# Attention with a position bias on one core: where the next batch's first stack stands in the DMA queue, and the softmax inversion one slot ahead

## The chip, the core and the metric

The kernel runs on one core of one Trainium2 chip. The metric is the device time of one launch in microseconds. The core has TensorE (PE), VectorE (DVE), ScalarE (ACT), GpSimd (POOL) and SyncE (SP), which issues nearly all transfers here, and 16 DMA engines that carry them.

## The reference

Sixteen batches of 512 tokens with 256 features go through a layer norm and then two branches, whose sum is added to x.

```python
xn = layernorm(x)                                   # (16, 512, 256)
q, k, v = split(xn @ w_qkv.T + b_qkv)               # 16 heads of 16
att = q @ k.T / 4 + hope_bias(pos_independent)      # per head, 512 x 512
att = softmax(where(causal, att, -inf))
attn = (att @ v) @ w_proj.T + b_proj
ffn = fp8_gemm(xn.astype(bf16), ffn_kernel)         # values rounded to float8_e4m3
out = x + attn + ffn
```

The bias of a head is a sum of cosines and sines of the distance i - j and a constant. It can therefore be written as a product of features of i and features of j, which the kernel stacks under q and k.

## The kernel before

**Stacks.** Each head has 64 rows in `STK`: high and low parts of q and k and the position features that belong to them. A *pair* of heads fills the 128 partitions of `STK[:, u]`, and a *stack* is the four heads (two pairs) of one group g of four. One transfer of 512 KB per pair copies it from 32 partitions of `QKP`, where the projections are written (line 365, `load_stack`, called once per batch and group; it signals `stack_loaded[g]` for both pairs).

**Units and slots.** A batch b has 4 units, one per group g, and a unit has 12 slots. In a slot PE does a tile of transposed scores of (b, g) (`scores_T`, line 629, and 632 for the position features of groups 0 and 1, kept in `EXT`) and, in turn with it, a tile of scores of the group two units further on (`scores`, line 606). The latter serve only to find the row maxima: DVE adds the causal mask and takes maxima (`chunk_max`, line 989). Twelve tiles later ACT rounds the maxima, PE turns them (line 590), ACT writes them as `neg_max_T` (line 830), and SP sends them, in four transfers of 4 KB, into two rows of each head's stack (line 328, `send_max`, `load_max`). So the transposed scores of (b, g) come out with the maximum already taken off, and ACT's exponential (line 911) writes the probabilities straight. POOL masks them (line 1187), PE multiplies them by V beside ones (line 655), so that the sums of the rows come along.

In unit 2 of batch b the scores ahead are those of (b+1, group 0). They need the next batch's first stack.

**Inversion.** The sums of all 16 heads are gathered in `DEN`. DVE inverts them in one instruction (line 996, `invert`) in unit 0 of the next batch, at the slot `INVERT_AT`, behind that slot's maxima. SP stores them to DRAM (`store_recips`, line 384), and reads them back spread over partitions (`spread_recips`, line 396, two transfers of 256 KB). POOL divides in unit 1.

**What sets the order.** Each engine's order is written out by hand: tables of (unit, slot) at the top of the file, and for SP the sequence in `body`. A queue is in order: SP waits for one condition, issues, and goes on. Within a batch SP does: the last stack of this batch, the maxima of group 1, `store_recips`, x for b+2, `spread_recips`, **the next batch's first stack, the maxima of group 2, the regrouping of `out_T` of group 0** (lines 341 and 342), the next batch's second stack, the maxima of group 3, and so on. The places where PE waits for it:

```python
# scores, at tile 0 of a unit
pe.wait_ge(stack_loaded[g], 32 * (b + 1))
# scores_T, at slot 0 of a unit
pe.wait_ge(max_loaded[g], 64 * (b + 1))
```

The first wait asks for both pairs of the stack (16 from each). In a slot the first transposed tile comes ahead of the tile of scores. At unit 2's slot 0 PE then does the quantised product (line 582).

Of the kernel before, what the change touches and what calls it, by code (L numbers as in the profile page):

```python
# [72 lines left out]
XH_AT, FIRST_XH_AT = [(3, 9), (3, 10)], [(0, 2), (0, 2)]  # L73
XL_AT, FIRST_XL_AT = [(3, 10), (0, 0)], [(0, 3), (0, 3)]

INVERT_AT, LAST_INVERT_AT = (0, 8), (3, 8)
STATS_AT, AGGR_AT = [(1, 2), (1, 3), (1, 5), (1, 8)], (1, 9)
MAGIC_AT = [(2, 0), (2, 1), (2, 2)]

# [48 lines left out]
def build(nc, x, w_qkv, b_qkv, w_proj, b_proj, pos, ffn_w, s_in, s_k, ffn_b, feat_q, feat_k, out):  # L128
    with ExitStack() as ctx:
# [196 lines left out]
        def send_max(eng, g):  # L326
            for h in range(HU):
                eng.dma_start(max_rows(g, h), MTS[2 * TT * h:2 * TT * h + 2 * TT, g % 2, :].bitcast(F32)) \  # L328
                    .then_inc(max_loaded[g], 16)

        def wait_alone(eng, always, *pairs):


            held = [(s, v if isinstance(v, int) else eng.compute_val(v)) for s, v in pairs]
            eng.wait_ge(*always)
            for s, v in held:
                eng.wait_ge(s, v)

        def send_attn(eng, b, g):
            r = 64 * (g % 2)  # L340
            eng.dma_start(attn_row(b)[r:r + HU * HD, g // 2, :], OT[0:P:2, :]).then_inc(ot_stored[g % 2], 16)
            eng.dma_start(DEN[32 * g:32 * g + 32, :], OT[1:P:2 * HD, :]).then_inc(den_loaded[g % 2], 16)
# [13 lines left out]
        def _(sp):  # L356
            def load_x(b):
                sp.dma_start(x_slot(b), x[bass.ds(b, 1), :, :].rearrange("o (t p) c -> p (o t) c", p=P)) \
                    .then_inc(x_loaded, 16)

            def load_stack(b, g):

                for u in (2 * g, 2 * g + 1):
                    r = 32 * (u % 4)
                    sp.dma_start(STK[:, u, :, :].bitcast(F32), QKP[r:r + 32, u // 4, :, :, :].bitcast(F32)) \
                        .then_inc(stack_loaded[g], 16)

            def load_max(b, g):
                sp.wait_ge(mts_ready, 4 * b + g + 1)
                send_max(sp, g)  # L370

            def regroup(b, g, early):

                if g == 0 and not early:

                    wait_alone(sp, (w_loaded, 16), (al_ready, b), (rc_ready, b), (ot_ready, 4 * b + g + 1))
                else:
                    sp.wait_ge(ot_ready, 4 * b + g + 1)
                send_attn(sp, b, g)

            def store_recips(b):

                wait_alone(sp, (w_loaded, 16), (rc_ready, b + 1), (rb_loaded, 32 * (b + 1)))
                sp.dma_start(recips.rearrange("h (e j) -> (h e) j", e=8), RDEN[:, :]).then_inc(rc_stored, 16)

            def spread_recips(b, last):

                if not last:

                    wait_alone(sp, (w_loaded, 16), (rc_stored, 16 * (b + 1)), (t_ready, 2 * (b + 3)))  # L390
                else:
                    sp.wait_ge(rc_stored, 16 * (b + 1))
                    sp.wait_ge(qm_done, 2 * B)
                for ct in range(CT):
                    src = recips[8 * ct:8 * ct + 8, :].unsqueeze(1).broadcast_to([8, HD, T])
                    sp.dma_start(RB[:, ct, :], src).then_inc(rb_loaded, 16)
# [50 lines left out]
            for u, loaded in enumerate((first_pair, stack_loaded[0])):  # L447
                sp.dma_start(STK[:, u, :, :].bitcast(F32), QKP[32 * u:32 * u + 32, 0, :, :, :].bitcast(F32)).then_inc(loaded, 16)
            load_stack(0, 1)
            sp.wait_ge(ql_ready, 4)  # L450
            sp.wait_ge(const_made, 2)
            load_stack(0, 2)
            load_low_features(1)

            def store_out(b):
                sp.wait_ge(out_ready, 2 * (b + 1))
                sp.dma_start(out[bass.ds(b - 1, 1), :, :].rearrange("o (t p) c -> p (o t) c", p=P),
                             x_slot(b + 3)).then_inc(out_stored, 16)

            def body(b, first, last, load):  # L460
                if not first:
                    sp.wait_ge(st_ready, ROW * b)
                load_stack(b, 3)
                load_max(b, 1)
                if not first:
                    store_recips(b - 1)
                if load:
                    if not first:
                        sp.wait_ge(out_stored, 16 * b)
                    sp.wait_ge(x_loaded, 16 * (b + 2))  # L470
                    load_x(b + 2)
                if not first:
                    spread_recips(b - 1, last)

                if not last:
                    wait_alone(sp, (w_loaded, 16), (st_ready, ROW * b + SLOTS),
                               (ql_ready, 4 * (b + 1) + 2))
                    load_stack(b + 1, 0)
                load_max(b, 2)
                regroup(b, 0, first)  # L480

                if not last:
                    wait_alone(sp, (w_loaded, 16), (st_ready, ROW * b + 2 * SLOTS))
                    load_stack(b + 1, 1)
                load_max(b, 3)
                regroup(b, 1, first)

                if not last:
                    wait_alone(sp, (w_loaded, 16), (st_ready, ROW * b + 3 * SLOTS),
                               (ql_ready, 4 * (b + 1) + 4))  # L490
                    load_stack(b + 1, 2)
                if not last:
                    load_max(b + 1, 0)
                regroup(b, 2, first)
                if not first and not last:
                    store_out(b)

            body(0, True, False, True)
            with sp.Fori(1, B - 2) as b:
                body(b, False, False, True)  # L500
            body(B - 2, False, False, False)
            body(B - 1, False, True, False)
            store_recips_of(0, 12, B)
# [846 lines left out]
```

## Time and profile before

| what | value |
|---|---|
| median of 3 runs | 822.24 us (822.04 to 825.26) |
| the profiled execution's own time | 820.26 us |
| its span, first to last instruction | 818.5 us |
| mean granted TensorE clock | 0.973 of full speed |
| PE busy | 747.2 us, 91% |
| DVE, ACT, POOL busy | 628.9, 581.0, 528.2 us |
| DMA, mean over the span | 130 GB/s |
| one batch, inversion to inversion | 46.4 to 47.6 us |

Busy time says how long an engine worked, not whether the work was on the path that sets the end. For that the profile has a chain of waits, followed back from the last instruction, and a list of who waited for whom. SP counts as a queue: the length of a DMA instruction on it is the time until the issue was accepted, and the time to landing is told apart.

### The profile page before, as it was taken

What the parts mean: (1) busy time and instruction counts of PE and PEld (TensorE: products, weight loads), DVE (VectorE), ACT (ScalarE), POOL (GpSimd) and SP (SyncE); (2) the same over time, 40 slices, a digit from 0 to 9 for tenths busy, and PEclk for the clock granted to TensorE, in tenths of its full rate; (3) what the DMA queues carried; (4) which work ended last, traced back from release to release, by engine and by line L of the source; (5) the groups of instructions that cost most, each with busy time, mean ns of one, the idle gap of its engine ahead of it and who ended that gap; (6) DMA issues with size and microseconds to landing.
All of it is one profiled execution on the core that took longest, in us unless ns stands there. A gap on an engine that the chain in (4) does not pass through costs nothing.

```text
span 818.5 us, 23154 instructions
## 1 busy us (share of the span) xinstructions
PE 747.2 (91%) x6313; PEld 510.0 (62%) x6313; DVE 628.9 (77%) x2395; ACT 581.0 (71%) x1258; POOL 528.2 (65%) x525
## 2 busy tenths in 40 slices
PE   6869999999999999999999999999999999999883
PEld 3546666666676667657676666657666666767552
DVE  3767878887977878788788878787787879778722
ACT  4236767777786877778687777778677777867671
POOL 6433568567666867667676757766685776667580
PEclk8859999999999999999999999999999999999998
DMA  6834666567566656666566657756665775666502
GB/s 170 165 68 95 114 145 123 129 148 144 127 138 153 118 130 138 138 145 137 141 121 151 123 127 162 142 126 137 148 117 123 155 143 124 139 130 121 120 24 86
DMA packets 55548, 106.07 MB, mean 130 GB/s; under 512 B 10464, under 2 KB 30432, under 8 KB 55520
## 3 DMA queue, kind: packets, MB, share of 16 engines
q1 hardware_dynamic: 53192, 102.96, 60.4%
q10 hardware_dynamic: 2328, 2.77, 1.0%
q8 instruction: 13, 0.21, 0.1%
q14 instruction: 15, 0.12, 0.0%
HBM read 18.68 MB, written 8.91 MB: 34 GB/s over the span
## 4 chain that ended last, share of the span: by engine, by line
PE 49%; ACT 15%; SPq 11%; issue 9%; DMA 7%; DVE 5%; ACTq 3%; DVEq 1%; POOL 0%; POOLq 0%
SPq L328 11%; PE misc_a L539 8%; PE misc_a L655 8%; PE scoreT_b L629 6%; PE misc_b L539 6%; ACT probs L911 6%; PE scoreT_a L629 3%; DMA stacks<-neg_max_T 3%; PE misc_b L655 3%; PE score_a L606 3%; PE score_c L606 2%; ACT qk_parts L818 2%; ACT out_T L884 2%; ACT attn_hi L893 2%; ACT xnT_hi L807 1%
## 5 line engine op out<-in xcount | busy, mean ns | idle before, releaser
L1187 POOL TENSOR_SCALAR_AFFINE_SELECT probs<-probs 128x512 f32<-128x512 f32 x256 | 159.5, 635 | 244.7 <-ACT probs L911 242.8
L989 DVE CUSTOM_DVE_ANT_0 score_b<-score_b,causal_mask_q 128x384 f32<-128x384 f32 (+3 forms) x321 | 161.9, 521 | 119.6 <-PE score_b L606 118.4
L989 DVE CUSTOM_DVE_ANT_0 score_a<-score_a,causal_mask_q 128x512 f32<-128x512 f32 x319 | 173.1, 559 | 8.1 <-PE score_a L606 4.1
L911 ACT ACTIVATE probs<-scoreT_b 128x384 f32<-128x384 f32 (+1 forms) x256 | 134.5, 525 | 60.7 <-issue 23.7
L989 DVE CUSTOM_DVE_ANT_0 score_c<-score_c,causal_mask_q 128x256 f32<-128x256 f32 (+3 forms) x384 | 171.4, 474 | 2.3 <-PE score_c L606 2.2
L911 ACT ACTIVATE probs<-scoreT_a 128x512 f32<-128x512 f32 (+1 forms) x256 | 145.6, 569 | 14.0 <-PE scoreT_a L632 7.4
L989 DVE DVE_READ_ACCUMULATOR2_ANT row_max<- 128x1 f32 x1024 | 142.9, 140 | 0.0
L911 ACT ACTIVATE probs<-scoreT_c 128x384 f32<-128x384 f32 (+1 forms) x256 | 136.2, 532 | 3.7 <-PE scoreT_c L632 3.3
L655 PE MATMUL misc_a<-probs,v_ones 128*32 128x128 f32 (+3 forms) x1536 | 131.2, 438 | 0.4 <-POOL probs L1187 0.4
L629 PE MATMUL scoreT_a<-stacks 64*128 64x512 f32 (+3 forms) x320 | 108.3, 358 | 21.8 <-DMA stacks<-neg_max_T 13.8
L629 PE MATMUL scoreT_b<-stacks 64*128 64x384 f32 (+3 forms) x320 | 119.5, 393 | 7.6 <-ACT probs L911 7.1
L606 PE MATMUL score_b<-stacks 64*128 64x384 f32 (+3 forms) x321 | 118.3, 401 | 0.3 <-DVE row_max L989 0.2
L629 PE MATMUL scoreT_c<-stacks 64*128 64x256 f32 (+3 forms) x384 | 105.7, 308 | 8.7 <-ACT probs L911 8.7
L606 PE MATMUL score_a<-stacks 64*128 64x512 f32 x319 | 108.5, 372 | 5.5 <-DVE row_max L989 4.0
L629 PEld LDWEIGHTS scoreT_b<-stacks 64*128 64x128 f32 x320 | 56.8, 185 | 73.5 <-ACT probs L911 42.5
L606 PE MATMUL score_c<-stacks 64*128 64x256 f32 (+3 forms) x384 | 99.2, 312 | 0.5 <-DVE row_max L989 0.2
L629 PEld LDWEIGHTS scoreT_c<-stacks 64*128 64x128 f32 x384 | 68.7, 186 | 16.0 <-ACT probs L911 14.1
L655 PEld LDWEIGHTS misc_a<-probs,v_ones 128*32 128x32 f32 x1536 | 59.7, 109 | 29.5 <-issue 13.3
L629 PEld LDWEIGHTS scoreT_a<-stacks 64*128 64x128 f32 x320 | 57.1, 186 | 30.8 <-DMA stacks<-neg_max_T 15.9
L606 PEld LDWEIGHTS score_a<-stacks 64*128 64x128 f32 x319 | 55.3, 188 | 22.1 <-DVE row_max L989 16.4
L606 PEld LDWEIGHTS score_c<-stacks 64*128 64x128 f32 x384 | 65.7, 189 | 5.1 <-DVE row_max L989 4.8
L884 ACT ACTIVATE out_T<-misc_a 128x512 f32<-128x512 f32 x48 | 28.7, 598 | 41.4 <-PE misc_a L655 39.8
(241 smaller groups left out, 1948.9 us busy)
## 6 DMA issues: line engine op xcount, KB each, us to landing
stacks<-qk_parts SPq DMA_DIRECT2D x128, 512.0 KB, 8.1
x_ring<-in_L_attn_x SPq DMA_DIRECT2D x16, 512.0 KB, 3.6
xn<-recips SPq DMA_DIRECT2D x31, 256.0 KB
out<-x_ring SPq DMA_DIRECT2D x15, 512.0 KB, 3.0
attn<-out_T SPq DMA_DIRECT2D x48, 128.0 KB, 2.6
stacks<-neg_max_T SPq DMA_DIRECT2D x128, 4.0 KB
attn<-out_T ACTq DMA_DIRECT2D x16, 128.0 KB, 2.9
low_features<-neg_max_T SPq DMA_DIRECT2D x124, 4.0 KB
```

Source lines behind the costliest of these rows:

```text
L328: eng.dma_start(max_rows(g, h), MTS[2 * TT * h:2 * TT * h + 2 * TT, g % 2, :].bitcast(F32)) \
L539: last = mm(o, l(ct), r(ct), start=(ct == 0 and i == 0), stop=(ct == CT - 1 and i == 2))
L606: last = mm(SB_[n % 3][:, o:o + w], STK[rows, u, 0, P * qt:P * qt + P], STK[rows, u, 1, 0:w], start=True, stop=True)
L629: last = mm(bank, STK[rows, u, 1, P * j:P * j + P], STK[rows, u, 0, P * j:T], start=True, stop=(g >= 2))
L655: last = mm(bank[32 * i:32 * i + 32, P * j:T], VA[:, j, HU * g + i, :, :].rearrange("p d a -> p (d a)"), probs(g, j)[:, i, :], start=(j == ...
L807: A(XH[:, ct, :], misc_of("T", ct)[:, :], ACT.Copy).then_inc(xh_ready, 1)
L818: A(qk_part(m, 0), misc_of("QK", m)[:, :].unsqueeze(1).broadcast_to([P, 2, T]), ACT.Identity, bias=BQ[:, bias:bias + 1]).then_inc(qh_ready, 1)
L884: A(OT[:, :], misc_of("PV", g)[:, :], ACT.Copy).then_inc(ot_ready, 1)
L893: A(AH[:, ct, :], attn_row(b)[:, ct, :], ACT.Copy).then_inc(ah_ready, 1)
L911: A(probs_slot(g, k), STB[(SLOTS * g + k) % 3][:, 0:w], ACT.Exp).then_inc(exp_done, 1)
L989: last = V.tensor_tensor_reduce(bank, bank, CMQ[:, T - w:T], 1.0, LEAST, ALU.add, ALU.max, MX[:, g % 2, 8 * h + 4 + qt:8 * h + 5 + qt])
L1187: last = GP.affine_select(out=d, in_=d, compare_op=ALU.is_ge, fill=0.0, base=0, pattern=[[0, HU], [1, P]], channel_multiplier=-1)
```

## The change

The next batch's first stack is sent in two steps. Its first pair (heads 0 and 1) goes where the stack went; the second pair (heads 2 and 3) goes behind the maxima of group 2. The condition on which the stack waited stands ahead of the first pair alone; PE's wait for both pairs is as before. In the last batch there is no next stack. And the inversion stands in slot 7 instead of slot 8 of unit 0, for all batches but the first.

```diff
-INVERT_AT, LAST_INVERT_AT = (0, 8), (3, 8)
+INVERT_AT, LAST_INVERT_AT = (0, 7), (3, 8)
...
-            def load_stack(b, g):
+            def load_stack(b, g, pairs=(0, 1)):
 
-                for u in (2 * g, 2 * g + 1):
+                for u in (2 * g + i for i in pairs):
                     r = 32 * (u % 4)
...
                 if not last:
                     wait_alone(sp, (w_loaded, 16), (st_ready, ROW * b + SLOTS),
                                (ql_ready, 4 * (b + 1) + 2))
-                    load_stack(b + 1, 0)
+                    load_stack(b + 1, 0, (0,))
                 load_max(b, 2)
+                if not last:
+                    load_stack(b + 1, 0, (1,))
                 regroup(b, 0, first)
```

SP's queue in the loop over the batches, from the spread of the inverses (`xn<-recips`) to the regrouping of `out_T`, before:

```order
L396 DMA xn<-recips 128x1x512 [waits xnT_in_psum,inverses_stored,qk_weights_loaded]
L396 DMA xn<-recips 128x1x512
L334 ISA
L365 DMA stacks<-qk_parts 128x1x1024 [waits qk_lo_written,scoresT_in_psum,qk_weights_loaded]
L365 DMA stacks<-qk_parts 128x1x1024
L369 REGISTER_ALU
L328 DMA stacks<-neg_max_T 2x4x128 [waits max_T_written]
L328 DMA stacks<-neg_max_T 2x4x128 x3
L334 REGISTER_ALU
L341 ISA [waits denominators_inverted,out_T_written,attn_lo_written,qk_weights_loaded]
L341 DMA attn<-out_T 64x512
```

and now:

```order
L396 DMA xn<-recips 128x1x512 [waits xnT_in_psum,inverses_stored,qk_weights_loaded]
L396 DMA xn<-recips 128x1x512
L334 ISA
L365 DMA stacks<-qk_parts 128x1x1024 [waits qk_lo_written,scoresT_in_psum,qk_weights_loaded]
L369 REGISTER_ALU
L328 DMA stacks<-neg_max_T 2x4x128 [waits max_T_written]
L328 DMA stacks<-neg_max_T 2x4x128 x3
L365 DMA stacks<-qk_parts 128x1x1024
L334 REGISTER_ALU
L341 ISA [waits denominators_inverted,out_T_written,attn_lo_written,qk_weights_loaded]
L341 DMA attn<-out_T 64x512
```

The second transfer of the stack moved behind the four of the maxima, and so behind their condition, `max_T_written`; nothing else moved on SP.

VectorE in unit 0 of the loop, from the low part of the first projection (`qk_parts`) on, before (each `ISA` pair is a tile of maxima and the reading of its result):

```order
L977 SCALAR_TENSOR_TENSOR qk_parts<-misc_a,b_qkv,qk_parts 128x512 [waits qk_hi_written]
L334 REGISTER_ALU
L989 ISA score_c,row_max<-score_c,causal_mask_q 128x256 [waits scores_in_psum,x_loaded]
L989 ISA row_max 128x1
L989 ISA score_c,row_max<-score_c,causal_mask_q 128x128
L989 ISA row_max 128x1
L995 REGISTER_ALU
L996 RECIPROCAL denominators_inv<-denominators 128x64 [waits denominators1_regrouped,denominators0_regrouped]
L334 REGISTER_ALU
L989 ISA score_a,row_max<-score_a,causal_mask_q 128x256 [waits scores_in_psum,x_loaded]
```

and now (two lines further down in the file):

```order
L979 SCALAR_TENSOR_TENSOR qk_parts<-misc_a,b_qkv,qk_parts 128x512 [waits qk_hi_written]
L997 REGISTER_ALU
L998 RECIPROCAL denominators_inv<-denominators 128x64 [waits denominators1_regrouped,denominators0_regrouped]
L334 REGISTER_ALU
L991 ISA score_c,row_max<-score_c,causal_mask_q 128x256 [waits scores_in_psum,x_loaded]
L991 ISA row_max 128x1
L991 ISA score_c,row_max<-score_c,causal_mask_q 128x128
L991 ISA row_max 128x1
L334 REGISTER_ALU
L991 ISA score_a,row_max<-score_a,causal_mask_q 128x256 [waits scores_in_psum,x_loaded]
```

The inversion passed the two tiles of slot 8 in bank score_c. PE, ACT and POOL have the order that they had.

## Rows read from the trace of the kernel before

**Rows 1.** The page's part 1: busy time, share of the span, instructions

```profile
PE 747.2 (91%) x6313; PEld 510.0 (62%) x6313; DVE 628.9 (77%) x2395; ACT 581.0 (71%) x1258; POOL 528.2 (65%) x525
```

**Rows 2.** The page's part 4: the chain that ended last, by line

```profile
SPq L328 11%; PE misc_a L539 8%; PE misc_a L655 8%; PE scoreT_b L629 6%; PE misc_b L539 6%; ACT probs L911 6%; PE scoreT_a L629 3%; DMA stacks<-neg_max_T 3%; PE misc_b L655 3%; PE score_a L606 3%; PE score_c L606 2%; ACT qk_parts L818 2%; ACT out_T L884 2%; ACT attn_hi L893 2%; ACT xnT_hi L807 1%
```

**Rows 3.** List of waits: who waited for whom, us in total, times, longest

```profile
PE scoreT_a L629 <- DMA stacks<-neg_max_T: 13.8, 15, 1.6
```

**Rows 4.** Timeline of VectorE, batch 4: start, us, engine, line, operation, tiles

```profile
253.44 0.42 DVE L989 CUSTOM_DVE_ANT_0 score_c<-score_c,causal_mask_q 128x256 f32<-128x256 f32 x1
...
254.03 0.55 DVE L996 RECIPROCAL denominators_inv<-denominators 128x64 f32<-128x64 f32 x1
...
255.70 0.74 DVE L977 SCALAR_TENSOR_TENSOR qk_parts<-misc_b,b_qkv,qk_parts 128x512 fp32r<-128x512 f32 x1
```

**Rows 5.** Timeline of SyncE's queue, batch 4: start, us for all issues of the row

```profile
256.17 1.34 SPq L396 DMA_DIRECT2D xn<-recips  x2
257.74 1.23 SPq L365 DMA_DIRECT2D stacks<-qk_parts  x2
259.30 7.02 SPq L328 DMA_DIRECT2D stacks<-neg_max_T  x4
...
268.14 1.27 SPq L365 DMA_DIRECT2D stacks<-qk_parts  x2
```

**Rows 6.** Timeline of SyncE's queue, a unit whose stack went out 5 us before

```profile
319.76 2.73 SPq L328 DMA_DIRECT2D stacks<-neg_max_T  x4
```

**Rows 7.** Windows, batch 4; last three columns: PEclk, DMA share, GB/s

```profile
255.50:263.50 8.00, 7.98 (x72) 4.85 (x72) 6.93 (x27) 5.10 (x13) 5.11 (x6) 1.00 0.85 217
263.50:265.50 2.00, 2.00 (x16) 1.47 (x13) 1.96 (x8) 1.67 (x4) 0.96 (x2) 1.00 0.84 166
269.00:272.00 3.00, 3.00 (x30) 1.55 (x33) 2.98 (x9) 2.90 (x7) 2.17 (x4) 1.00 0.83 97
272.00:276.00 4.00, 3.84 (x46) 3.00 (x40) 2.55 (x9) 3.23 (x8) 3.00 (x2) 1.00 0.93 187
```

**Rows 8.** Timeline of TensorE at unit 2's start, batch 4; idle time in brackets

```profile
267.45 0.49 PE L629 MATMUL scoreT_a<-stacks 64*128 64x512 f32 x1 [0.94 <-DMA stacks<-neg_max_T]
267.63 0.49 PE L606 MATMUL score_a<-stacks 64*128 64x512 f32 x1
```

**Rows 9.** Issue to landing of the pairs from 257.74 and from 268.14 (longest: second)

```profile
DMA to landing us min/median/max: 7.3/7.9/8.5
...
DMA to landing us min/median/max: 7.0/7.6/8.2
```

**Rows 10.** Timeline of TensorE at unit 2's start, batches 5 and 6

```profile
314.06 0.50 PE L629 MATMUL scoreT_a<-stacks 64*128 64x512 f32 x1 [0.23 <-DMA stacks<-neg_max_T]
...
361.84 0.49 PE L629 MATMUL scoreT_a<-stacks 64*128 64x512 f32 x1 [1.58 <-DMA stacks<-neg_max_T]
```

**Rows 11.** Timeline of VectorE: the inversions of batches 5, 6 and 7

```profile
301.36 0.55 DVE L996 RECIPROCAL denominators_inv<-denominators 128x64 f32<-128x64 f32 x1
...
347.78 0.55 DVE L996 RECIPROCAL denominators_inv<-denominators 128x64 f32<-128x64 f32 x1
...
395.38 0.55 DVE L996 RECIPROCAL denominators_inv<-denominators 128x64 f32<-128x64 f32 x1
```

**Rows 12.** Timeline of ScalarE's queue, batch 4: the last denominators' issue

```profile
249.69 0.67 ACTq L342 DMA_DIRECT2D denominators<-out_T  x1
```

**Rows 13.** The page's part 6: issues, KB each, median us to landing

```profile
attn<-out_T ACTq DMA_DIRECT2D x16, 128.0 KB, 2.9
```

**Rows 14.** Timeline of TensorE behind the inversion, batch 4

```profile
254.51 0.33 PE L606 MATMUL score_c<-stacks 64*128 64x256 f32 x1
...
255.26 0.50 PE L606 MATMUL score_a<-stacks 64*128 64x512 f32 x1
```

**Rows 15.** Timeline of SyncE's queue, first batch: the maxima of unit 2

```profile
71.90 4.90 SPq L328 DMA_DIRECT2D stacks<-neg_max_T  x4
```

**Rows 16.** Timeline of TensorE at unit 2's start, first batch

```profile
79.07 0.47 PE L606 MATMUL score_a<-stacks 64*128 64x512 f32 x1
```

## Prediction

> **What bounds the kernel now.** The page's first lines: PE is busy 91% of the span, DVE 77%, ACT 71% [rows 1]. PE is the engine to watch, and its idle time is what a change of order can win or lose. The chain that ended last has SP's issue of the maxima (line 328) as its largest single line, 11% of the span, and the landing of the maxima with 3% [rows 2]. So the chain runs through the DMA queue once per batch. The list of waits says where PE feels it: its first transposed-score matmul of a unit waited for the landing of `stacks<-neg_max_T` 15 times, 13.8 us in all, 1.6 us at most, some 0.9 us per batch [rows 3].
>
> I take batch 4 as the example (of 0 to 15), whose inversion starts at 254.03, since its wait (0.94 us) is nearest that mean. In order: the DVE inversion at 254.03 [rows 4]; then SP stores the inverses, loads x, spreads the inverses at 256.17, issues both pairs of the next batch's first stack from 257.74, and the four maxima from 259.30, when ACT has written them. Those four issues take 7.02 us, until 266.32 [rows 5]. Where less is ahead of them, the same four take 2.73 us [rows 6]. So 4.3 us are SP standing still because what it issued before has not drained. Meanwhile the DMA engines move 217 GB/s until 263.5, and 166 GB/s in the next 2 us [rows 7]. PE finishes unit 1 at about 266.5 (267.45 less 0.94 of idling), starts unit 2's first transposed scores at 267.45 and next batch's first scores at 267.63 [rows 8]. These last need both pairs of the stack: the second pair, issued 0.64 us behind 257.74, landed 8.5 us later, at 266.9 [rows 9]. **Two things end within 0.6 us of each other at unit 2's start: the second pair (266.9) and the maxima (267.4).** Taking one away uncovers the other.
>
> **What an offset there is worth.** The trace has its own experiment. From the inversion to unit 2's first matmul it took 12.70 us in one batch (301.36 to 314.06) and 14.06 us in the next (347.78 to 361.84). The distances to the following inversions were 46.42 and 47.60 us [rows 10, 11]. So 1.36 us later there cost 1.18 us of the batch: 0.87 us per us. I use this rate in both directions.
>
> **The change, term by term.**
>
> *Inversion one slot ahead.* It now stands before the two tiles of score_c instead of behind them. It starts at 253.44 instead of 254.03, 0.59 us sooner [rows 4]. What it waits for, the last denominators, were issued at 249.69 [rows 12]; the transfer that is issued together with them lands after 2.9 us [rows 13], which gives 252.6, so it does not wait. The two tiles of score_c end 0.55 us later. PE's scores in that bank, at 254.51 [rows 14], wait until about 254.75. The next PE start that depends on DVE, score_a at 255.26, follows the tiles of score_a, whose end doesn't move. Cost nothing, as long as that cover of 0.5 us stands; without it, up to 0.25 us per batch. Behind it SP's store, spread and the first pair go 0.59 us sooner, the first pair at 257.15. The parts it copies are written by DVE at 255.70 + 0.74 [rows 4], before that.
>
> *The maxima ahead of the second pair.* They are ready at 259.29 as before. Ahead of them there is half a megabyte less. Unhindered they are issued by 259.30 + 2.73 = 262.0. At worst SP stands until the first pair too has drained. From 255.5 to 263.5 the engines moved 8 x 217 = 1736 KB [rows 7]; x, the inverses' spread and one pair are 524 KB each and some 60 KB come besides, so the first pair has drained near 263.0 now and will have near 262.4; the last of four short issues then ends by 264.0. Either way the maxima land before PE wants them at 266.5: the wait of [rows 3] is gone, worth up to 0.94 us here.
>
> *The second pair behind the maxima.* This is the price. Its issue moves from 258.4 to between 262.1 and 264.0. How long does a pair alone take? The trace never shows one: they always go two at a time. Bounds: two pairs from a clean start, issued at 268.14 and 0.65 us later, landed the second 8.2 us after its own issue, 8.85 us after the first's [rows 5, 9]. In them the engines moved 97 GB/s in the first 3 us and 187 GB/s in the next 4 [rows 7]. Taking off one pair at the later rate, 524 KB / 187 GB/s = 2.8 us, leaves **6.0 us** for a pair with a clean start. If it runs at the 217 GB/s of the busy stretch from its first packet (2.4 us), with the 0.9 us before the first packet and 0.3 us behind the last, it is **3.6 us**. I take 6.0, because by 262.4 the engines have nothing else left and the slow first 3 us came back whenever a pair started on idle engines. And I take the early issue, 262.1, because half a megabyte less stands ahead. Landing 268.1, next batch's first scores at 268.2 instead of 267.63: **0.6 us later.** The lowest and highest pairs of bounds give 265.7 (then PE's own arrival decides, 266.5 + 0.2) and 270.0: from 0.9 us sooner to 2.5 us later. Behind the stall nothing catches up: PE's quantised product (line 582) is next in PE's order, and ACT's read-out of it follows.
>
> The price by the Trainium skill: "SBUF — State Buffer", section "Door 1: The DMA port swizzle", says that what DMA can move depends on how many of the 16 SBUF ports the partitions reach, that 32 partitions in a row reach 8 of them, and that each port gives about 27.2 GB/s. A pair is read from 32 partitions, so by an estimate from that page it never moves faster than 217 GB/s, 2.4 us for a pair. The trace's 217 GB/s of the busy stretch agrees with it (with x in it, which is not read from there); its 97 GB/s in the first 3 us is under half of it, and the page gives no reason. By the page alone the pair would take about 3.6 us and the result would be the second rival's.
>
> *Fourteen batches* (1 to 14): 14 x 0.6 x 0.87 = 7.3 us. *Batch 0* has the split without the inversion: maxima at 71.90 [rows 15], second pair at 71.90 + 2.73 = 74.7, landed at 80.7, where PE took these scores at 79.07 without having waited [rows 16]: 1.6 us, 1.4 us of time. *Batch 15* has only the earlier inversion: nothing. The regrouping of out_T goes out some 3 us earlier; no wait of it is among the long ones, so I give it nothing. **Sum +8.7 us on the profiled execution's 820.26, 829.0.** The median of the runs shown is 2 us above that execution, so for a median about **831 us**, 1.1% slower.
>
> **Rivals.** A measurement of this kernel tells 0.5% (4.1 us) from no change.
>
> *A. The second pair becomes the wait (my forecast), chance 0.42.* 831 us. For: 8.2 and 8.5 us from the second pair's issue to its landing [rows 9]. Against: the time includes a neighbour's traffic.
>
> *B. The engines stay busy through the swap, chance 0.28, faster.* If the first pair and the second meet in the queues as now, the same bytes end 0.59 us sooner and the order inside them costs nothing. The second pair lands at 266.3 or before and PE goes on at once: 14 x 0.93 x 0.87 = 11.3 us less, 811; if half of it, 816. The point from which it decides: issue to landing under 5.0 us for the second pair (262.1 + 5.0 + 0.1 = 267.2, 0.4 sooner). For: 217 GB/s until 263.5 now [rows 7]. Against: a fast engine is out of work when the second pair arrives 0.9 us behind its issue.
>
> *C. The two cancel, chance 0.20.* Landing near 267.5: 822, within 0.5%.
>
> *D. SP still stands at the maxima, chance 0.10.* Issue at 264.0 and 6.0 us on: 270.0, 2.5 us later; 14 x 2.5 x 0.87 + 1.4 = 32 us, 854; at 1.5 us later it is 842.
>
> **Numbers.** Slower by over 0.5%: A and D, 0.52. Within: C, 0.20. Faster: B, 0.28. The range takes B's middle and A's bounds up to D's near end: 812 to 843; A's own is 826 to 838.
>
> **What would show it.** In the changed profile: (1) the inversion 0.6 us before the score_c tiles' old place, SP's chain with it; (2) the four maxima's issue near 2.7 us instead of 7; (3) the waits of PE's first transposed scores on `stacks<-neg_max_T` gone; (4) PE's score_a at unit 2's start idle on `stacks<-qk_parts`, some 1.5 us 14 times; (5) a pair issued alone taking about 6 us. I am wrong if (4) is under 0.5 us or a lone pair lands in under 5 us (B), or if (2) stays at 5 us or more (D).

## The result and the profile after

The changed kernel takes 876.0 us (873.3 to 883.1) against 823.75 us before (the table of before has three of these four runs): a ratio of 1.064 (interval 1.056 to 1.072). That is 52 us slower, or 3.7 us for each of the fourteen batches 1 to 14. The forecast was 831 us with 843 as its upper end. The direction was right, the size was about a sixth of what was measured (8.7 us of 52).

The page of the changed kernel, parts 1 and 4, with the row of granted clock from part 2 (lines of the file are two further down than before from `load_stack` on):

```profile
PE 775.0 (89%) x6313; PEld 520.9 (60%) x6313; DVE 629.8 (72%) x2395; ACT 580.6 (67%) x1258; POOL 522.7 (60%) x525
...
PEclk9779989989998999999999898999999999999897
...
DMA stacks<-qk_parts 12%; PE misc_a L657 10%; PE misc_a L541 7%; PE misc_b L541 6%; PE scoreT_b L631 6%; SPq L328 6%; ACT probs L913 5%; PE score_a L608 3%; PE scoreT_a L631 3%; PE misc_b L657 3%; PE score_c L608 2%; ACT xnT_hi L809 2%; ACT out_T L886 2%; ACT qk_parts L820 2%; PE misc_a L584 1%
```

Against [rows 1], DVE and ACT did the same work, but PE was busy 28 us longer with the same 6313 matmuls. Against [rows 2], the landing of the stack has come into the chain with 12%, more than SP's issue of the maxima lost. The waits, answering to [rows 3]:

```profile
ACT xnT_bf L939 <- PE misc_a L584: 46.0, 15, 4.6
PE score_a L608 <- DMA stacks<-qk_parts: 43.0, 16, 4.0
DVE score_a L991 <- PE score_a L608: 31.1, 16, 3.2
```

PE's wait for `stacks<-neg_max_T` has shrunk from 13.8 us in 15 times to 0.8 us, once. In its place PE waits 16 times for the pair, 2.7 us each, and ACT waits for PE's quantised product behind it. The timeline of batch 4, first SP's queue (answers to [rows 5]), then VectorE around the inversion (to [rows 4]), then TensorE at unit 2's start (to [rows 8]):

```profile
262.79 1.33 SPq L396 DMA_DIRECT2D xn<-recips  x2
264.35 0.59 SPq L365 DMA_DIRECT2D stacks<-qk_parts  x1
266.55 4.58 SPq L328 DMA_DIRECT2D stacks<-neg_max_T  x4
271.17 0.61 SPq L365 DMA_DIRECT2D stacks<-qk_parts  x1
```

```profile
259.99 0.75 DVE L979 SCALAR_TENSOR_TENSOR qk_parts<-misc_a,b_qkv,qk_parts 128x512 fp32r<-128x512 f32 x1 [0.46 <-ACT qk_parts L820]
260.66 0.54 DVE L998 RECIPROCAL denominators_inv<-denominators 128x64 f32<-128x64 f32 x1
```

```profile
273.59 0.44 PE L631 MATMUL scoreT_a<-stacks 64*128 64x512 f32 x1
278.00 0.79 PE L608 MATMUL score_a<-stacks 64*128 64x512 f32 x1 [3.97 <-DMA stacks<-qk_parts]
278.72 1.03 PE L584 MATMUL misc_a<-ffn_w_q,xq 128*128 128x256 bf16 x4
```

From issue to landing of that second pair (DMA issues, that one alone):

```profile
DMA to landing us min/median/max: 6.7/6.7/6.7
```

The second pair is issued 10.51 us behind the inversion (260.66 to 271.17) and lands at 277.9. PE stood still for 3.97 us. Batch 4 is the extreme case: over batches 1 to 14 of this trace the pair is issued 9.5 us behind the inversion on average (8.7 to 10.5), and PE stands still for 2.9 us (1.98 to 3.97). And what it does then is slow: score_a takes 0.79 us, against 0.49 in [rows 8], and the four matmuls of the quantised product 1.03 us. The windows of the same batch show why (columns: stretch and its length, busy us with instructions of PE, PEld, DVE, ACT and POOL, granted clock, DMA share, GB/s):

```profile
274.00:278.00 4.00, 0.03 (x2) 0.01 (x1) 1.75 (x9) 1.31 (x4) 3.55 (x7) 0.99 0.76 133
278.00:282.00 4.00, 4.00 (x15) 2.12 (x15) 1.80 (x4) 1.32 (x3) 0.04 (x1) 0.50 0.98 150
```

PE was busy for 0.03 of 4 us, and in the next 4 us its granted clock is 0.50: 1.2 GHz, not 2.4. Over the steady part of the run, 100 to 790 us, before and after:

```profile
100.00:790.00 690.00, 652.45 (x5721) 447.24 (x5721) 554.94 (x2139) 523.71 (x1141) 470.94 (x449) 1.00 0.64 133
```

```profile
100.00:790.00 690.00, 631.08 (x5306) 425.90 (x5307) 524.01 (x2003) 486.56 (x1057) 433.62 (x420) 0.96 0.63 127
```

A mean clock of 0.96 means that 0.04 / 0.5 = 8% of the time, some 55 us, ran at half speed. In the same stretch before, none did.

### The profile page after: what moved, and what is told of

Same layout as the page of the kernel before. It is cut to its first block, busy times and chain, and to the rows that moved or that the text cites. A ratio compares the mean times of both kernels' runs of the same rounds, so it can differ in the third digit from the quotient of the medians.

```text
span 871.9 us, 23154 instructions
## 1 busy us (share of the span) xinstructions
PE 775.0 (89%) x6313; PEld 520.9 (60%) x6313; DVE 629.8 (72%) x2395; ACT 580.6 (67%) x1258; POOL 522.7 (60%) x525
## 4 chain that ended last, share of the span: by engine, by line
PE 49%; DMA 15%; ACT 13%; issue 8%; SPq 6%; DVE 4%; ACTq 3%; DVEq 1%; POOL 0%; POOLq 0%
DMA stacks<-qk_parts 12%; PE misc_a L657 10%; PE misc_a L541 7%; PE misc_b L541 6%; PE scoreT_b L631 6%; SPq L328 6%; ACT probs L913 5%; PE score_a L608 3%; PE scoreT_a L631 3%; PE misc_b L657 3%; PE score_c L608 2%; ACT xnT_hi L809 2%; ACT out_T L886 2%; ACT qk_parts L820 2%; PE misc_a L584 1%
## 5 line engine op out<-in xcount | busy, mean ns | idle before, releaser
L608 PE MATMUL score_a<-stacks 64*128 64x512 f32 x319 | 112.1, 383 | 45.9 <-DMA stacks<-qk_parts 43.0
L991 DVE DVE_READ_ACCUMULATOR2_ANT row_max<- 128x1 f32 x1024 | 145.9, 142 | 0.0
L657 PE MATMUL misc_a<-probs,v_ones 128*32 128x128 f32 (+3 forms) x1536 | 137.9, 456 | 0.4 <-POOL probs L1189 0.4
L631 PE MATMUL scoreT_b<-stacks 64*128 64x384 f32 (+3 forms) x320 | 123.4, 405 | 8.0 <-ACT probs L913 7.9
L608 PE MATMUL score_b<-stacks 64*128 64x384 f32 (+3 forms) x321 | 121.9, 412 | 0.3 <-DVE row_max L991 0.2
L631 PE MATMUL scoreT_c<-stacks 64*128 64x256 f32 (+3 forms) x384 | 109.1, 315 | 8.8 <-ACT probs L913 8.8
L631 PE MATMUL scoreT_a<-stacks 64*128 64x512 f32 (+3 forms) x320 | 110.6, 365 | 5.9 <-DMA low_features<-neg_max_T 3.3
L608 PE MATMUL score_c<-stacks 64*128 64x256 f32 (+3 forms) x384 | 102.3, 320 | 2.1 <-DVE row_max L991 1.7
L608 PEld LDWEIGHTS score_a<-stacks 64*128 64x128 f32 x319 | 57.6, 195 | 64.2 <-DVE row_max L991 28.7
L631 PEld LDWEIGHTS scoreT_a<-stacks 64*128 64x128 f32 x320 | 59.3, 193 | 13.6 <-issue 7.7
```

The source lines that it names most:

```text
L608: last = mm(SB_[n % 3][:, o:o + w], STK[rows, u, 0, P * qt:P * qt + P], STK[rows, u, 1, 0:w], start=True, stop=True)
L631: last = mm(bank, STK[rows, u, 1, P * j:P * j + P], STK[rows, u, 0, P * j:T], start=True, stop=(g >= 2))
L657: last = mm(bank[32 * i:32 * i + 32, P * j:T], VA[:, j, HU * g + i, :, :].rearrange("p d a -> p (d a)"), probs(g, j)[:, i, :], start=(j == ...
L991: last = V.tensor_tensor_reduce(bank, bank, CMQ[:, T - w:T], 1.0, LEAST, ALU.add, ALU.max, MX[:, g % 2, 8 * h + 4 + qt:8 * h + 5 + qt])
```

## The experiments

The theory after this reading had two parts: the pair comes too late for PE, and the standing still costs PE its clock as well. Each run below was timed beside the kernel before.

**Inversion alone.**

```diff
-INVERT_AT, LAST_INVERT_AT = (0, 8), (3, 8)
+INVERT_AT, LAST_INVERT_AT = (0, 7), (3, 8)
```

> The inversion moves from slot 8 to slot 7, and the stack stays in one piece ahead of the maxima. Theory (the late second pair does all the harm): SP's chain goes 0.6 us sooner, second pair and maxima land 0.6 us sooner, TensorE's wait for the maxima at unit 2 falls from 13.8 us to about 6 us over the batches, and the time falls by about 14 x 0.6 x 0.87 = 7 us, to 816. Rival (the inversion in slot 7 delays VectorE's tiles and with them TensorE): slower than before by several us, 828 or more.

Measured: 818.5 us, ratio 0.993 (0.990 to 0.996). The waits for the maxima at unit 2:

```profile
PEld scoreT_a L629 <- DMA stacks<-neg_max_T: 5.9, 11, 1.0
PE scoreT_a L629 <- DMA stacks<-neg_max_T: 4.1, 8, 0.8
```

From 13.8 us in [rows 3] to 4.1. The inversion's move is a gain of about 6 us by itself, as the prediction had it. All of the harm, and more, is the split.

**Split alone.** The changed kernel with `INVERT_AT` back at (0, 8).

> The stack is split around the maxima, the inversion stays in slot 8. Theory: the second pair is issued and lands about when it does in the changed kernel or up to 0.6 us later, so 876 to 885 us, with the granted clock again at half after the waits. Rival (the inversion does a part of the harm): below 870.

Measured: 889.0 us, ratio 1.080 (1.073 to 1.087), a little above the expected range. The wait in its list:

```profile
PE score_a L608 <- DMA stacks<-qk_parts: 51.6, 16, 4.5
```

PE waits 3.2 us per batch, against 2.7, and the kernel takes 13 us more than with the inversion ahead. So the inversion's move brings twice as much beside the split as alone. PE's waits account for 8.6 of the 13 us (51.6 less 43.0); where the rest is lost was not taken apart.

**TensorE waits by pair.** The changed kernel; the first pair signals `first_pair`, and PE waits for the second only where it reads it. ScalarE's own wait for the two pairs names both signals.

```diff
-                if c == 0 and not early:
-                    pe.wait_ge(stack_loaded[g], 32 * (b + 1))
+                if c == 0 and not early:
+                    pe.wait_ge(*((stack_loaded[g], 32 * (b + 1)) if g else (first_pair, 16 * (b + 1))))
+                if c == 2 and g == 0 and not early:
+                    pe.wait_ge(stack_loaded[0], 16 * (b + 1))
```

> The changed kernel's order, but TensorE waits for the first pair at tile 0 and for the second pair only at tile 2, which is the first tile that reads it. Theory: tile 2 comes some 3 us behind tile 0, near 16.0 us after the inversion, and the second pair lands at 16.2, so of the 2.9 us per batch at most 0.5 remains, the clock stays at full, and the time is 815 to 830. Rival (the cost lies in SP's queue or in the DMA traffic that the new order makes, not in TensorE's one wait): above 850.

Measured: 828.7 us, ratio 1.006 (1.002 to 1.010). PE's waits for the stack, in the list of waits:

```profile
PEld score_c L609 <- DMA stacks<-qk_parts: 11.5, 11, 1.8
PE score_c L609 <- DMA stacks<-qk_parts: 6.8, 9, 1.4
```

Same queue, same late transfer, same traffic, and 47 us of the 52 are gone. So the harm is made at one place, PE's wait for both pairs at tile 0. It is still 10 us slower than the inversion alone. The new wait in its list is the one that is left at tile 2 (6.8 us on the matmuls, 11.5 on their weight loads); that this makes up the 10 us was not tested.

**The wait filled with matmuls.** The changed kernel; between the wait for the bank and that for the stack, PE does nine matmuls (`FILL`) with weights of zero into the bank that the scores overwrite. They take no part in the result.

```diff
-                if c == 0 and not early:
+                if c == 0 and g and not early:
                     pe.wait_ge(stack_loaded[g], 32 * (b + 1))
...
+                if c == 0 and g == 0 and not early:
+                    for _ in range(FILL):
+                        mm(SB_[n % 3][:, :], CMQ[:, 0:P], CMQ[:, :], start=True, stop=True)
+                    pe.wait_ge(stack_loaded[g], 32 * (b + 1))
```

> The changed kernel, with nine matmuls of zeros (128x512 bf16, some 0.2 us each at full clock) into the bank that the next tile of scores overwrites, between the wait for the bank and the wait for the stack. They compute nothing that is used. Theory (a part of the harm is the granted clock, which falls to half after TensorE has stood still): the clock stays at full in most batches and the time falls by 15 to 28 us, to 850 to 861, while the second pair lands as late as before. Rival (the clock has another cause): 876 and more, clock 0.94 as now.

Measured: 856.3 us, ratio 1.041 (1.034 to 1.048). The pair still lands 6.7 us behind its issue:

```profile
DMA to landing us min/median/max: 6.7/6.7/6.7
```

Timeline of PE around unit 2's start in batch 4, then the windows of the same place:

```profile
275.07 1.89 PE L608 MATMUL score_a<-causal_mask_q 128*128 128x512 bf16 x8 [0.16 <-issue]
278.52 0.50 PE L613 MATMUL score_a<-stacks 64*128 64x512 f32 x1 [1.56 <-DMA stacks<-qk_parts]
```

```profile
274.50:278.50 4.00, 2.30 (x13) 0.90 (x10) 2.13 (x14) 1.69 (x4) 3.64 (x6) 1.00 0.76 132
278.50:282.50 4.00, 3.98 (x34) 2.13 (x38) 3.21 (x9) 2.73 (x6) 0.34 (x2) 1.00 0.94 140
```

The pair comes as late, but the clock stays at 1.00, score_a takes 0.50 us again, and useless work makes the kernel 20 us faster. The added matmuls ended 1.56 us before the pair landed, so here they held nothing up. Nor did they in another of the fourteen batches: PE's wait for the pair is left in each, 0.19 us at least. Over 100 to 790 us the mean clock is back at 1.00:

```profile
100.00:790.00 690.00, 655.21 (x5600) 441.47 (x5616) 539.13 (x2066) 500.91 (x1090) 445.95 (x431) 1.00 0.65 129
```

The clock's part of the 52 us is so about 20 us; the other 32 us come with the lateness itself.

**Old order, waits by pair.** The kernel before with the edit of the third experiment.

> The kernel before, with TensorE's wait split: first pair at tile 0, second pair at tile 2. Theory: before the change the maxima landed last, some 0.5 us behind the second pair, and the order of the queue stays, so the wait for the pair hid nothing: the time stays within 0.5% of before, 820 to 827. Rival (the wait for the second pair already cost something before): faster than 818.

Measured: 823.6 us, ratio 0.996 (0.993 to 0.999). Within the expected range. Before the change the maxima were the last to land; that PE asked for both pairs at once cost about 0.4% (0.1 to 0.7%).

**Inversion ahead and an earlier x.** The inversion alone, with `load_x` ahead of `store_recips` in SP's order (the same edit as in the next experiment).

> The inversion in slot 7, the old order of the stack, and x for two batches on loaded while SP waits for the inversion, not behind it. Theory: half a megabyte less is in the engines when the inverses' spread and the stack come, maxima and second pair land 1 us sooner, TensorE's remaining wait for the maxima (about 0.25 us per batch after the inversion alone) goes: 811 to 816. Rival (x there collides with the previous stack's tail and delays the denominators, and with them the inversion): 820 or more.

Measured: 817.25 us, ratio 0.990 (0.987 to 0.993). That is above the expected range, and the interval overlaps that of the inversion alone. Its row in the list of waits:

```profile
PE scoreT_a L629 <- DMA stacks<-neg_max_T: 4.9, 8, 1.1
```

The row is no shorter than the 4.1 us of the inversion alone, and the expected gain did not show. Half a megabyte of x ahead in the queue was not what held the maxima.

**Changed kernel and an earlier x.** The same edit on the changed kernel.

```diff
                 load_max(b, 1)
-                if not first:
-                    store_recips(b - 1)
                 if load:
...
+                if not first:
+                    store_recips(b - 1)
                 if not first:
                     spread_recips(b - 1, last)
```

> The changed kernel with the same early x. Theory (the harm is the second pair's late issue and its own 6.7 us to land on idle engines): the issues of the maxima are no longer held up and the second pair is issued near 8.7 us behind the inversion instead of 9.5, it lands near 15.4 instead of 16.2, TensorE still waits some 2 us per batch: 855 to 868, half of the clock loss remaining. Rival (the harm is the crowd ahead of it in the queue): below 835.

Measured: 880.0 us, ratio 1.065 (1.059 to 1.071), as slow as the changed kernel; the expected gain of 8 us or more failed. SP's queue in batch 4:

```profile
268.90 0.59 SPq L365 DMA_DIRECT2D stacks<-qk_parts  x1
271.06 3.29 SPq L328 DMA_DIRECT2D stacks<-neg_max_T  x4
274.40 0.61 SPq L365 DMA_DIRECT2D stacks<-qk_parts  x1
```

The maxima start 2.16 us behind the pair, as in the changed kernel (264.35 to 266.55); their issue shrank from 4.58 to 3.29 us here, but PE's wait in all from 43.0 to 40.2 us only, and the mean clock from 100 to 790 us was 0.95. So x, the part of the crowd ahead that this experiment moves, is not the cause. The inverses' spread and the first pair are still ahead, and their part was not tested. What remains is SP's order: the pair cannot go before the maxima are ready and issued.

**Second pair from ScalarE.** The changed kernel; ACT issues the second pair before unit 1's first exponential, and SP no longer does.

```diff
-                if not last:
-                    load_stack(b + 1, 0, (1,))
...
+                        if (g, k) == (1, 0) and not last:
+                            act.wait_ge(ql_ready, 4 * (b + 1) + 2)
+                            act.dma_start(STK[:, 1, :, :].bitcast(F32), QKP[32:64, 0, :, :, :].bitcast(F32)) \
+                                .then_inc(stack_loaded[0], 16)
```

> The changed kernel, with the second pair issued by ScalarE at unit 1's first slot instead of by SP behind the maxima. Theory (the late issue is the cause, not that the stack goes in two steps): the second pair is issued some 5 us sooner and lands within 13 us of the inversion as before the change, the maxima behind the first pair alone land sooner, and TensorE's wait at unit 2 is under 0.5 us per batch: 812 to 822. Rival (the splitting itself costs, through two queues or ScalarE's time): above 830.

Measured: 829.8 us, ratio 1.005 (1.002 to 1.008). The theory's main point holds: with the pair issued early the 52 us shrink to 4. But 829.8 is above the expected range and 0.2 us short of the rival's. PE waited for the maxima again, 1.3 us each time (list of waits):

```profile
PE scoreT_a L629 <- DMA stacks<-neg_max_T: 8.9, 7, 1.9
```

SP's queue in batch 4, then the landing of the first pair that it issues there (DMA issues, that one alone):

```profile
257.14 0.59 SPq L365 DMA_DIRECT2D stacks<-qk_parts  x1
259.50 5.19 SPq L328 DMA_DIRECT2D stacks<-neg_max_T  x4
```

```profile
DMA to landing us min/median/max: 9.0/9.0/9.0
```

In SP's queue the maxima have the same ahead of them as in the changed kernel. Yet the first pair takes 9.0 us where it took 6.4 there, and the issue of the maxima 5.19 us instead of 4.58 (means over batches 1 to 14: 5.0 and 3.5 us). So a pair in ScalarE's queue still stands in the way of what SP issues; how the two share the engines stays open.

**Why a pair alone takes 6.7 us.** Two experiments of one run each. In the first the second pair goes as two transfers, each from 16 partitions to 64, and all waits for the stack count one transfer more:

```diff
-                    load_stack(b + 1, 0, (1,))
+                    for i in range(2):
+                        sp.dma_start(STK[64 * i:64 * i + 64, 1, :, :].bitcast(F32),
+                                     QKP[32 + 16 * i:48 + 16 * i, 0, :, :, :].bitcast(F32)) \
+                            .then_inc(stack_loaded[0], 16)
```

> The changed kernel, the second pair sent as two transfers of 64 partitions each, one behind the other. What it asks is why a pair alone takes 6.7 us from issue to landing. Theory (the first 3 us are slow because all engines start together on the same few source partitions, and two transfers start the same way): the pair lands 6.5 us or more behind its first issue, the time stays at 870 to 885. Rival (the time is that of the longest queue of one transfer, and two shorter ones spread better): landed under 6 us, 860 or less.

Measured: 877.3 us in one run. The halves, issued at 272.96 and 0.66 us later (DMA issues, these two):

```profile
DMA to landing us min/median/max: 4.3/5.0/5.7
```

The second landed 5.7 us behind its own issue, 6.4 behind the first's: 0.3 us sooner than in one piece. That lies between the theory's 6.5 and the rival's 6 and settles little; the time is the theory's. In the second experiment the regrouping goes ahead of the pair:

```diff
                 load_max(b, 2)
+                regroup(b, 0, first)
                 if not last:
                     load_stack(b + 1, 0, (1,))
-                regroup(b, 0, first)
```

> The changed kernel, with the regrouping of out_T (128 KB and the sums) ahead of the second pair instead of 0.4 us behind it. Theory (a pair takes 6.7 us on idle engines by itself): issued 1.2 us later and landing 6.5 to 6.8 us behind its issue, 885 to 900 us. Rival (the regrouping's packets between its own make it slow): it lands under 6.2 us behind its issue, and the time is 870 to 885.

Measured: 905.9 us in one run, above both ranges. In batch 4 the pair, issued at 282.36, landed after

```profile
DMA to landing us min/median/max: 6.1/6.1/6.1
```

which is the rival's figure. But batch 4 is one of the quickest. In batch 3, where the next stack is issued 1.2 us behind the pair and not 2.9 us, it took

```profile
DMA to landing us min/median/max: 6.9/6.9/6.9
```

The time fits neither, since the issue came later still, and PE waited longer (list of waits):

```profile
PE score_a L608 <- DMA stacks<-qk_parts: 65.7, 16, 5.8
```

So traffic close behind a pair may hold it up by some 0.6 us, and about 6 us are left with nothing close behind it; two single runs do not show more. Why it starts slowly stays open. The Trainium skill ("SBUF — State Buffer", "Door 1: The DMA port swizzle") lists 104 GB/s, measured on transfers of 1 MiB, where the partitions reach four ports; the first 3 us moved 97 [rows 7], but that the engines start on four ports was not tried.

## Why the prediction was right or wrong

**What bounds the kernel.** Right. The second pair and the maxima ended within 0.6 us of each other, and taking one away uncovered the other: the pair here, the maxima where ScalarE sends the pair.

**Inversion one slot ahead.** Right in mechanism and size. It follows the projection's low part directly (259.99 + 0.75 to 260.66, overlapping) and waits for nothing. Alone it brings 6 us, where 14 x 0.59 x 0.87 makes 7.

**The maxima ahead.** Right that the wait for them would go. Their issue was taken as 2.73 us; in batch 4 it is 4.58 (above), 1.9 us more, in batch 5 it is 2.73 (SP's queue, changed kernel):

```profile
319.64 2.73 SPq L328 DMA_DIRECT2D stacks<-neg_max_T  x4
```

The bound from the first pair's draining, 264.0, corresponds to 4.7 us, and batch 4 lies there. Over batches 1 to 14 the mean is 3.5 us, so a value between the bounds was the one to take. TensorE at the start of unit 2 in that batch 5, the shortest wait:

```profile
329.11 0.77 PE L608 MATMUL score_a<-stacks 64*128 64x512 f32 x1 [1.98 <-DMA stacks<-qk_parts]
329.81 1.03 PE L584 MATMUL misc_a<-ffn_w_q,xq 128*128 128x256 bf16 x4
```

**The second pair behind the maxima.** The right rival (A), but here is the first step that failed: the offset of 0.6 us was mis-sized, by both of its terms. The pair took 6.7 us from issue to landing instead of 6.0, and its issue was taken at the early bound. In batch 4 the next scores start 17.3 us behind the inversion (260.66 to 278.00); the prediction had 268.2 - 253.44 = 14.8. Of the 2.5 us, 1.9 are the issue and 0.7 the landing. Over batches 1 to 14 the mean is 16.3 us, 1.5 us later than forecast: the offset was 2.1 us and not 0.6. At the prediction's own rate that is 14 x 1.5 x 0.87 = 18 of the 43 us that its sum lacks. The wait was named as a sign at 1.5 us; it was 2.9 in these batches (and 1.9 in batch 0, where 1.6 was forecast). Rival B had said that the engines stay busy, and a pair then takes 3.6 us. No run showed a whole pair under 5.9 us, not even the first pair of the changed kernel, which joins engines at work (6.4 us in batch 4). Rival D had the price of standing at the maxima, 2.5 us and 854 us. That is near the 856 us of the filled wait, where the offset was 2.3 us, and it misses the result by the clock's part.

**What an offset there is worth.** This is the second step that failed, as large as the first: the clock was put at nothing. The rate of 0.87 us per us came from [rows 10, 11], two batches in which PE stood still for 0.23 and 1.58 us, and in both the granted clock stayed at full. In the changed kernel it falls behind the shortest wait too, as the rows above show: 1.98 us idle, then 0.77 us for a matmul of 0.49. The filled wait prices it at 20 of the 52 us. The trace before held a warning, though not a price. Its clock is full only from batch 1 to the last batch. In the third of 40 slices the mean is down to 0.5 (part 2 of the page, row of the clock), and near the end, where PE stands still for 6.98 us, it is 0.50 again (windows, then TensorE's timeline):

```profile
PEclk8859999999999999999999999999999999999998
```

```profile
804.70:811.40 6.70, 2.90 (x12) 2.64 (x12) 1.93 (x3) 0.63 (x1) 0.00 (x0) 0.50 0.28 88
```

```profile
808.29 0.55 PE L776 MATMUL scoreT_a<-w_projT_hi,attn_hi 128*128 128x256 f32 x1 [6.98 <-DVE attn_lo L1137]
```

The Trainium skill names this loss ("TensorE: Matmul & The Clock Gate", "HAM oscillation — how this bites in real kernels"): in the kernel that it describes, the wait for DMA in every round costs the clock in every round. The prediction did not weigh it, though it forecast a wait for DMA in every batch. The trace after agrees with the page for 12 of its 14 batches.

**The time without the clock.** 856 - 824 = 32 us, about 2.2 us per batch. In the trace of the filled wait the next scores start 16.5 us behind the inversion on average, against 13.6 before. Less the 0.59 us by which the inversion went ahead, that is 2.3 us later in the batch, and a batch takes 49.33 us instead of 47.11, 2.2 us more. So without the clock an offset costs nearly its full length, by an estimate from these two traces, where the prediction had 0.87. The 43 us that the sum lacks are then 18 for the size of the offset, 20 for the clock, and 5 of which the higher rate would make some 3; no run tests these 5. The scores start 0.2 us later there than in the changed kernel, so the clock's part may be a little over 20.

## What to carry to other kernels

Before a transfer is moved behind others, ask which is the first instruction that waits for it, and whether it needs all of it: the same queue cost 52 us with one wait for both pairs and 5 us with a wait for each. A rate taken from small offsets holds as far as those offsets went; where a change makes TensorE stand still longer than in any batch before, ask what the half clock would cost behind it, and look for it at the start and the end of the trace too. And test the parts of a change apart: here one of them was a gain of 6 us that the other hid.

## What the runs showed of the hardware

TensorE's granted clock fell to 0.50 behind idle times of 1.98 and 3.97 us in the changed kernel. In batch 4 it is 0.50 for the 4 us from 278 on (windows above), and the mean of the 8 us that follow is 0.83:

```profile
282.00:290.00 8.00, 7.85 (x70) 5.17 (x69) 5.04 (x17) 5.88 (x14) 3.07 (x3) 0.83 0.29 68
```

The length of the standstill alone does not decide it. In the steady part of the trace before, with 1.58 us at most at this wait, the mean clock was 1.00. But in the changed kernel it stayed at 1.00 in two of the fourteen batches, with 2.04 and 2.37 us of idle time. The second of them, TensorE's timeline and the windows:

```profile
633.95 0.49 PE L608 MATMUL score_a<-stacks 64*128 64x512 f32 x1 [2.37 <-DMA stacks<-qk_parts]
```

```profile
633.95:641.95 8.00, 7.85 (x71) 5.06 (x73) 6.15 (x17) 5.99 (x14) 4.84 (x6) 1.00 0.74 126
```

And where ScalarE sends the second pair it fell once behind 1.39 us:

```profile
502.85 0.57 PE L629 MATMUL scoreT_a<-stacks 64*128 64x512 f32 x1 [1.39 <-DMA stacks<-neg_max_T]
```

```profile
502.85:506.85 4.00, 4.00 (x16) 2.26 (x16) 2.28 (x8) 1.80 (x4) 3.73 (x7) 0.57 1.00 147
```

With useless matmuls in the gap, and 0.2 to 2.0 us idle behind them, it stayed at 1.00 in all fourteen batches. What PE had done before each of these gaps was not varied.

A transfer of 512 KB between partitions of the same core took 6.6 to 6.9 us from issue to landing as the late pair of the changed kernel, with only 128 KB close behind it. That is hardly less than the 7.0 and 7.3 us of the first of two that go together [rows 9]. And SP can stand still at the issue of a 4 KB transfer: four of them took 2.73 us or 4.58 us with the same work ahead, and 7.02 us with one pair more ahead [rows 5].
